# A gated-attention and FFN block on one core: a new opening that computes all six modulation rows, with both halves of x loaded ahead of the first two modulation matrices

## What is computed

```python
mod = (silu(c) @ wmod).reshape(4, 6, 1, 512)
sa, ca, ga, sb, cb, gb = (mod[:, i] for i in range(6))
ga, gb = ((2 * (g >= 0) - 1) * maximum(abs(g), 0.25) for g in (ga, gb))
h = layernorm(x) * (1 + ca) + sa
x = x + ga * attention(h)
h = layernorm(x) * (1 + cb) + sb
x = x + gb * (silu(h @ w_gate.T) * (h @ w_up.T)) @ w_down.T
```

## Time and profile before

| what | value |
|---|---|
| runs | 1098.33, 1099.9, 1103.17 us |
| the profiled execution's own time | 1100.45 us |
| its span, first to last instruction | 1098.7 us |
| busy in the span | PE 1045.7, DVE 816.6, ACT 696.6, POOL 224.2 us |
| first `scores` of the loop | 78.58 us from the start |
| first transpose of the FFN stage | 897.18 us from the start |
| DMA | 70.89 MB, 65 GB/s over the span |

### The profile page before, as it was taken

How to read it: one execution, slowest core, us unless ns; L and a number is a source line. 1 busy time by engine, 2 the same in 40 slices (tenths; PEclk the granted TensorE clock), 3 DMA queues, 4 the chain that set the end, 5 groups by cost and what they waited for, 6 DMA issues and landing times. The chain is left out here.

```text
span 1098.7 us, 14605 instructions
## 1 busy us (share of the span) xinstructions
PE 1045.7 (95%) x4680; PEld 808.4 (74%) x4680; DVE 816.6 (74%) x1585; ACT 696.6 (63%) x1368; POOL 224.2 (20%) x140
## 2 busy tenths in 40 slices
PE   5879999999999999999999999999997859999898
PEld 1657777777777777877777777787774349888786
DVE  5777887888888788878888887887878785444412
ACT  3448877887787788778878787877874434222300
POOL 3412212222211131122222112211323410000000
PEclk9989999999999999999999999999998969999999
DMA  6122301310131122013101311220123231111011
GB/s 226 55 67 80 112 20 38 100 53 19 38 115 39 33 85 91 19 38 115 38 19 38 126 44 40 77 76 19 45 72 135 76 129 45 57 38 58 29 39 38
DMA packets 37464, 70.89 MB, mean 65 GB/s; under 512 B 2936, under 2 KB 19576, under 8 KB 35520
## 3 DMA queue, kind: packets, MB, share of 16 engines
q1 hardware_dynamic: 36720, 70.16, 19.8%
q10 hardware_dynamic: 720, 0.43, 0.1%
HBM read 68.33 MB, written 2.24 MB: 64 GB/s over the span
## 5 line engine op out<-in xcount | busy, mean ns | idle before, releaser
L1373 POOL TENSOR_TENSOR q_sin<-q_sin,cst 128x512 f32<-128x512 f32 x64 | 88.9, 1388 | 311.7 <-ACT q_sin L764 311.7
L1213 DVE SCALAR_TENSOR_TENSOR prob<-ps_s,scal,dec 128x128 f32<-128x128 f32 x256 | 71.9, 343 | 77.6 <-PE ps_s L670 77.6
L1361 POOL TENSOR_TENSOR dec<-dec,future 128x1024 f32<-128x1024 f32 x31 | 74.5, 2402 | 265.9 <-ACT expg L783 265.9
L54 PE MATMUL ps_q<-hT_hi,wq_hi 128*128 128x512 f32 x256 | 125.5, 490 | 3.3 <-DVE q_cos L1023 2.5
L54 PE MATMUL ps_o<-wo_hi,z_hi 128*128 128x512 f32 x260 | 103.8, 399 | 2.5 <-DVE z_lo L49 2.4
L54 PE MATMUL ps_gt<-hT_hi,wg_hi 128*128 128x512 f32 x256 | 103.8, 405 | 2.0 <-DVE sg L1043 2.0
L56 PE MATMUL ps_o<-wo_hi,z_lo 128*128 128x512 f32 x260 | 103.4, 398 | 0.0
L55 PE MATMUL ps_o<-wo_lo,z_hi 128*128 128x512 f32 x260 | 103.2, 397 | 0.0
L56 PE MATMUL ps_q<-hT_hi,wq_lo 128*128 128x512 f32 x256 | 101.2, 395 | 0.0
L55 PE MATMUL ps_gt<-hT_lo,wg_hi 128*128 128x512 f32 x256 | 101.1, 395 | 0.0
L56 PE MATMUL ps_gt<-hT_hi,wg_lo 128*128 128x512 f32 x256 | 100.7, 393 | 0.0
(11 more groups left out here) (251 smaller groups left out, 2737.6 us busy)
## 6 DMA issues: line engine op xcount, KB each, us to landing
dec<-gT_dram SPq DMA_DIRECT2D x32, 512.0 KB, 5.5
raw_q<-wq_in SPq DMA_DIRECT2D x32, 256.0 KB, 2.7
raw_g<-wg_in SPq DMA_DIRECT2D x32, 256.0 KB, 2.9
raw_o<-wo_in SPq DMA_DIRECT2D x8, 1024.0 KB, 6.9
raw_pair<-wkv_in SPq DMA_DIRECT2D x8, 512.0 KB, 4.7
raw_pair<-wgu_in SPq DMA_DIRECT2D x6, 512.0 KB, 3.2
raw_gu<-wgu_in SPq DMA_DIRECT2D x5, 512.0 KB, 3.4
qT<-wmod_in SPq DMA_DIRECT2D x2, 1024.0 KB, 6.9
```

Source lines behind the costliest of these rows:

```text
L54: pe.matmul(out, w_hi, x_hi, start=first, stop=False)
L1213: last = nc.vector.scalar_tensor_tensor(prob[:, h], ps_s[:, h * P:(h + 1) * P], scal[:, tile, 1, h:h + 1], dec[:, tile // 2 % 2, h, tile % ...
L1361: nc.gpsimd.tensor_tensor(cells, cells, future[:].unsqueeze(1).broadcast_to([P, GRP * CPB, CHUNK]), ALU.add).then_inc(mask_done, 1)
L1373: nc.gpsimd.tensor_tensor(q2, q2, sinT, ALU.mult).then_inc(qsin_done, 1)
```

## The change

The tail's four rows and `guard_gate` go, and all six rows are made in the opening, in the order SA, CA, SB, CB, GA, GB. Each of a row's four k slices goes to its own strip of 32 result partitions; ACT copies the whole 128 x 512 bank, and `mod_turn` multiplies it with a 128 x 4 selector, which sums the strips and turns them. The norm works by batches: one ACT instruction covers both tiles of a batch, lower parts of batches 0 and 1 are made by POOL, of 2 and 3 by DVE. Heads 0 to 3 get own buffers (`raw_first`), their upper parts go to ACT, their lower parts stay on DVE. The two softplus products stand ahead of the first q block, and the whole softplus series stands ahead of `gate(0, -4)`. The zeroing of the output weights (3.7 us in the profile, L1379 to L1381) and of x1 by POOL stands behind the heads' splits and the last row. ga is stored and x reloaded before POOL needs them. The gates are stored to HBM element by element.

```diff
@@ SP
             sp.dma_start(cT, cT_in).then_inc(c_loaded, 16)
-            for half, m in enumerate((SA, CA)):
-                load_mod(m)
-                a = half * NT // 2
-                sp.dma_start(x1[:, a:a + NT // 2], ...
+            load_x(0)
+            load_x(1)
+            load_mod(SA)
+            load_mod(CA)
             load_kv(0)
-            load_head(0, 0, True)
+            load_first(0)
             sp.dma_start(cst[:, C_COST:C_TRI], cst_in[:, C_COST:C_TRI]).then_inc(tables_loaded, 16)
-            for j in range(1, GRP):
-                load_head(0, j)
+            load_first(1)
+            load_mod(SB)
+            load_mod(CB)
+            load_first(2)
+            load_first(3)
+            sp.wait_ge(ln_turned, B)
+            load_mod(GA)
+            load_mod(GB)
...
+            sp.wait_ge(guard, GUARD_END)
+            for i in range(2):
+                sp.dma_start(modrow[i].rearrange("(m p) -> p m", p=P),
+                             gate_T[:, i].rearrange("p b k -> p (b k)"),
+                             allow_slow_non_contiguous=True).then_inc(rows_stored, 16)
...
                     step(g, t, False, True, False)
                     sp.wait_ge(zz_done, g * 8 + 4)
-                    load_mod(CB)
-                    load_mod(SB)
+                    (loads both halves of x_again)
@@ PE
+            def mod_rows(m):
+                pe.wait_ge(mod_loaded[m], 16)
+                for k in range(KT):
+                    nc.tensor.matmul(ps_rows[m][k * LANE:(k + 1) * LANE], silu_c[:, k], wmod[m][:, k],
+                                     start=True, stop=True).then_inc(rows_ready, 1)
+            def mod_turn(slot, count):
+                pe.wait_ge(rows_copied, count)
+                part = mod_part[(count - 1) % 2]
+                for k in range(KT):
+                    last = nc.tensor.matmul(ps_modT[:, slot, k], part[:, k * P:(k + 1) * P], sel,
+                                            start=True, stop=True)
+                last.then_inc(mod_turned, 1)
...
+            mod_rows(SA); mod_rows(CA)
+            ln_turn(0); mod_turn(0, 1); mod_turn(1, 2); ln_turn(1)
+            kv_chunk(0, -1, 0); ln_turn(2); kv_chunk(0, -1, 1); ln_turn(3)
+            softplus_argument(0); softplus_argument(1)
+            q_block(0, -4, True); k_turn(0, -1); g_block(0, -4, 0, KT, True)
+            softplus_turn()
+            q_block(0, -3); mod_rows(SB); mod_turn(2, 3)
+            g_block(0, -3, 0, KT); mod_rows(CB); mod_turn(3, 4)
+            cumulative()
+            q_block(0, -2); mod_rows(GA); mod_turn(4, 5)
+            g_block(0, -2, 0, KT); mod_rows(GB); mod_turn(5, 6)
+            q_block(0, -1); g_block(0, -1, 0, KT)
@@ PE tail
-                    mod_row(GA)
-                    mod_row(CB)
-                    mod_row(GB)
-                    mod_row(SB)
-                    mod_turn(ps_late_modT, late_rows, 4)
@@ ACT, order from the first keys on
+            copy_zT(0); copy_v(0, -1); copy_zT(1)
+            swap(0, -4, True); copy_kT(0, -1); exp_gate(0, -4)
+            nc.scalar.activation(za, za, ACT.Exp, scale=-1.0)
+            sigmoid(0, -4); first_hi(2); swap(0, -3)
+            copy_rows(SB); exp_gate(0, -3); sigmoid(0, -3)
+            copy_rows(CB); first_hi(3); (copies of cumulative's results)
+            swap(0, -2); copy_rows(GA); exp_gate(0, -2); sigmoid(0, -2); copy_rows(GB)
@@ DVE, order from the norm on
+            ln_hi_half(0); split_kv_hi(0); split_kv_lo(0)
+            ln_tile_stats(6); ln_tile_stats(7); ln_variance(3)
+            ln_normalise(2); ln_hi_half(1); ln_normalise(3); first_lo(0)
+            for b in range(2, B):
+                ln_hi_half(b)
+                ln_lo_half(b)
+            split_v_lo(0, -1); rotate_k(0, -1); first_lo(1)
+            rotate_q_cos(0, -4); softplus_before_exp(); rotate_q_add(0, -4); cap(0, -4)
+            softplus_argument_of_series(); softplus_series(0); softplus_series(1)
+            gate(0, -4); decay_rates(); first_lo(2)
+            rotate_q_cos(0, -3); late_modT(2, 0.0); rotate_q_add(0, -3); cap(0, -3); gate(0, -3)
+            late_modT(3, 1.0); chunk_end(); first_lo(3)
+            (the same for -2, then state_weight, copy_scalars, guard_gates, the mask, then -1)
@@ DVE tail
-                    guard_gate(0)
-                    guard_gate(1)
@@ POOL
+            for t in range(-4, -1):
+                rotate_q_sin(0, t)
+            pool.wait_ge(wh_split, GRP)
+            (zeroes wo_hi, wo_lo)
+            pool.wait_ge(rows_ready, KT * len(MODS))
+            nc.gpsimd.memset(x1[:], 0.0).then_inc(zeros_done, 1)
+            rotate_q_sin(0, -1)
+            def residual_tile(t):
+                pool.wait_ge(sums_done, KVH * NT - (NT - 1) + t + 1)
+                scale_sum(nc.gpsimd, 0, t)
+                add_x(nc.gpsimd, pool, 0, t, t)
```

More of the change, by code:

```diff
@@ L39 @@
 SA, CA, GA, SB, CB, GB = range(6)
+MODS = (SA, CA, SB, CB, GA, GB)
 def split_hi(engine, hi, full):
@@ L418, in load_mod, with load_x, load_first, load_head @@
             def load_mod(m):
[L419 to L427, removed]
+                sp.dma_start(wmod[m], wmod_in[m]).then_inc(mod_loaded[m], 16)
+            def load_x(half):
+                a = half * NT // 2
+                sp.dma_start(x1[:, a:a + NT // 2], x_in[a:a + NT // 2].rearrange("t p n -> p t n"))\
+                    .then_inc(x_loaded[half], 16)
+            def load_first(j):
+                sp.dma_start(raw_first[:, j, 0], wq_in[j]).then_inc(first_loaded[j], 16)
+                sp.dma_start(raw_first[:, j, 1], wg_in[j]).then_inc(first_loaded[j], 16)
+            def load_head(g, j):
+                sp.wait_ge(wh_split, g * 4 + j)
                 sp.dma_start(raw_q[:], wq_in[bass.ds(g * 4 + j, 1)].rearrange("o p k d -> (o p) k d"))\
@@ new lines, in mod_turn, with ln_turn @@
+                last.then_inc(mod_turned, 1)
+            def ln_turn(b):
+                pe.wait_ge(ln_xn, CPB * (b + 1))
+                if b >= 2:
+                    pe.wait_ge(ln_hf, b - 1)
+                for c in range(CPB):
+                    for k in range(KT):
+                        last = nc.tensor.transpose(pairs[b % 2][:, c, k * P:(k + 1) * P],
+                                                   x1[:, b * CPB + c, k * P:(k + 1) * P], ident)
+                last.then_inc(ln_turned, 1)
@@ new lines, in _ @@
+            scalar_rstd(2)
+            first_hi(0)
+            scalar_rstd(3)
+            modulate(2)
+            modulate(3)
+            first_hi(1)
+            copy_zT(0)
+            copy_v(0, -1)
+            copy_zT(1)
+            swap(0, -4, True)
+            copy_kT(0, -1)
+            exp_gate(0, -4)
+            act.wait_ge(chain, CHAIN_ABS)
+            nc.scalar.activation(za, za, ACT.Exp, scale=-1.0).then_inc(exp_done, 1)
+            sigmoid(0, -4)
+            first_hi(2)
@@ L859, in _ @@
+            swap(0, -2)
+            copy_rows(GA)
+            exp_gate(0, -2)
+            sigmoid(0, -2)
+            copy_rows(GB)
+            act.wait_ge(chain, CHAIN_DIFF)
+            nc.scalar.activation(zs, zs, ACT.Exp).then_inc(exp_done, 1)
+            act.wait_ge(mod_turned, 6)
+            exp_g(0, -1)
+            swap(0, -1)
+            decays(0, 0)
+            exp_gate(0, -1)
+            sigmoid(0, -1)
             act.wait_ge(gT_stored, 32)
@@ L1157, in _ @@
[L1157 to L1166 removed]
+            ln_tile_stats(6)
@@ new lines, in _ @@
+            first_lo(1)
+            rotate_q_cos(0, -4)
+            softplus_before_exp()
+            rotate_q_add(0, -4)
+            cap(0, -4)
+            softplus_argument_of_series()
+            softplus_series(0)
+            softplus_series(1)
+            gate(0, -4)
+            decay_rates()
+            first_lo(2)
+            rotate_q_cos(0, -3)
+            late_modT(2, 0.0)
+            rotate_q_add(0, -3)
+            cap(0, -3)
+            gate(0, -3)
+            late_modT(3, 1.0)
@@ new lines, in _ @@
+            chunk_end()
+            first_lo(3)
+            rotate_q_cos(0, -2)
+            rotate_q_add(0, -2)
+            cap(0, -2)
+            gate(0, -2)
+            state_weight()
+            copy_scalars(0, -1, True)
+            guard_gates()
+            dve.wait_ge(expg_done, 1)
+            dve.wait_ge(future_done, 2)
+            cells = dec[:, 0].rearrange("p h c i -> p (h c) i")
+            nc.vector.tensor_tensor(cells, cells,
+                                    future[:].unsqueeze(1).broadcast_to([P, GRP * CPB, CHUNK]),
+                                    ALU.add).then_inc(mask_done, 1)
@@ L1205, in _ @@
+            rotate_q_cos(0, -1)
+            rotate_q_add(0, -1)
+            cap(0, -1)
             dve.wait_ge(zeros_done, 1)
```

505 lines of the change are left out of this document (241 added, 264 removed).

## The result

The changed kernel took 1123.8 us (median of 4 runs, 1122.65 to 1125.59) against 1099.1 of the kernel before on the same chips: ratio 1.0222, 95% interval 1.0187 to 1.0257. The forecast was 1108.5, the range ended at 1118.

The account below looks back on a forecast made before the run. PE is busy throughout the loop, so only the opening and the last group's tiles 4 to 7 could move time: 1100.45 + 9.4 - 1.0 = 1108.9, forecast as 1108.5 us; own range 1105.5 to 1113, wide range 1098 to 1118.

Parts of the forecast that it names:

- wide range: Whole kernel: 1098 to 1118 us, taking in rivals of a break-even opening and serial strips, and the unknowns' ends.
- own range: Whole kernel: the forecast's narrower range, 1105.5 to 1113 us around 1108.5.
- Leg 1: Opening, from 0 to the first modulation: wmod[CA] lands later, strips run together; modulation at 21.6, 1.9 us later than before.
- rival 3: Row strips run one after the other instead of beside each other: +6 us, 1114.5; chance 0.17.
- Leg 2: Opening, up to the softplus turn: wkv_lo ends at 28.0 against 24.65 before; chain ends at 48.7 us.
- Leg 3: Opening, up to g_block(0, -3): it waits for gate(0, -4) behind the whole series, starts at 58.2; PE idles some 5 us.
- Leg 4: Opening, up to the end of cumulative: gate block, CB's selector product after ACT, cumulative sums; ends at 67.7 us.
- Leg 5: Opening, up to scores: remaining q and gate blocks, rows GA and GB; 18.1 us, ending at 85.8.
- my term for it: Opening: matmuls at the lower clock behind three waits of 2 us or more, 2.2 us; scores at 88.0.
- The zeroing of x1: Opening, near the cap of t = -2: POOL's zeroing may add up to 3 us, left to the range.
- Tail: Last group's tiles 4 to 7: taken rows return 3.0 us, lower clock costs 2.0, net -1.0; ends -5 to +2.
- Rival 4: Element-wise gate stores hold the queue: +5 us in the loop's first steps, 1113.9; chance 0.08.

Follow-up runs that it names:

- a1: Kernel before with 32 unused bytes a partition behind the constants table, moving the left SBUF tensors up 32 bytes; 1110.0 us, ratio 1.0077.
- a2: Changed kernel with 224 unused bytes a partition behind the constants table, restoring left tensors' addresses modulo 256; 1113.9 us, ratio 1.0118 to before.
- m1: Matmuls alone in the kernel's shapes, weights and moving operand each at four addresses 32 bytes apart; 226.9 to 234.3 ns from start to start.
- b1: a2 plus unneeded matmuls in PE's waits in the opening; 1112.2 us, ratio 1.0122 to the kernel before.
- c2: c1 with each late selector product behind the next block of products and the fillers ahead of them gone; 1112.1 us, ratio 1.0102 to before.
- d4: c1 without rows SB, CB, GA, GB, their copies, selector products and the gates' bound, ones instead; 1106.8 us, ratio 1.0067 to before.
- c3: Kernel before plus unneeded matmuls in its own PE waits in opening and tail; 1098.0 us, ratio 0.9976.
- b4: a2 plus unneeded matmuls in PE's waits in the last group's tiles 4 to 7; 1107.1 us, ratio 1.0075 to the kernel before.
- d1: c2 with gate stores on ACT's queue, x1 zeroed behind the cap of t = -2, z 128 bytes higher; 1106.2 us, ratio 1.0061 to before.
- e2: d1 with the two element-wise gate stores issued by SP in the last group's first step; 1098.9 us, ratio 0.9995 to the kernel before.
- b2: a2 with gate(0, -4) on DVE moved ahead of the softplus series; 1117.3 us, ratio 1.0166 to the kernel before.
- c1: a2 with the gate order of b2, tail fillers of b4 and fewer opening fillers than b1; 1105.4 us, ratio 1.0052 to the kernel before.

## Why the prediction was wrong, step by step

- **"... the loop's instructions are the same after the change, so it can move the time only through the opening ..., the last group's tiles 4 to 7 ... and nothing behind": this step failed.** The same instructions ran 5.3 us slower in the loop and 5.1 in the FFN stage, because their operands had moved by 32 bytes (a1, a2, m1). Without them the time is a2's 1113.9: inside the wide range, 5.4 above the forecast and 0.9 above the end of its own range.
- Leg 1 held: modulation at 21.97 (21.6). Four matmuls of a row run beside each other: 1.06 us warm against 3.60, 3.4 times; rival 3 is out. The Trainium skill ("TensorE: Matmul & The Clock Gate", Part 3, "Measured speedup vs the span model") has 2.38 times for three strips; no run here has three, and four gave more.
- Leg 2 held: wkv_lo ended at 28.52 (28.0), the softplus turn began at 48.81 (48.7). Its sum enters 2.6 for a lower part priced at 2.4; that changes nothing.
- Leg 3: g_block(0, -3) at 59.56 (58.2), behind gate(0, -4) with 4.5 us of idle PE around the selector product. The six series operations took 3.78, not some 2.7. The sum itself is loose here: it enters 1.3 for operations listed with 1.2 and 0.4, and adds the 0.9 that it calls beside; from the turn to the argument's first operation (48.81 to 51.59) it was 2.8 instead of these 2.2.
- Leg 4: 11.7 us instead of 9.5. The gate block ran 4.6 instead of 2.8 at the lower clock; the rest fits.
- Leg 5: 22.3 instead of 18.1: the last q block 5.3 instead of 2.8, the selector product 1.4 instead of 0.8, small terms more. Low clock in legs 4 and 5 was 5 us by these rows and 4.7 by b1, and my term for it 2.2: the largest mis-sized term of the opening, half of its 5.6 over the forecast.
- The zeroing of x1, left to the range at up to 3, missed the cap in the changed kernel by 0.1 us; that it cost nothing was luck. It made the cap 4.8 (c2) and 6.1 (d4) longer where it met it.
- Tail: the mechanism was right, both sizes were not. With fillers in both kernels the tail is 67.8 (c3) and 62.1 (b4), so the rows and their collateral were worth 5.7 us, not 3.0 (of that up to 2.4 is row CB at the lower clock, 5.97 for 3.60). The lower clock cost the changed kernel 7.2 (5.4 against a2) and the kernel before 1.7, so the change added 5.5 (3.7), not 2.0. That -0.3 lies near the forecast's -1.0 is luck: two errors of like size cancel. By the Trainium skill's rule ("TensorE: Matmul & The Clock Gate", "Loop structure matters more than you think") I had +2.2; the trace agrees with the rule's direction, output and square-sum products at 0.77 behind waits of 3 to 6 us, and b4 shows the price.
- Rival 4's mechanism exists (c2, d1, e2), its price was zero here, 1.7 us in b1 and 5.7 in c2, whose openings are shorter.

## What to carry to other kernels

"The same instructions" are the same only if their operands stay where they were: after any edit to a buffer's size, compare the length of a stretch that should not change first. Work that is taken out of PE's waits can be paid back in clock unless something else keeps PE busy. A change in order should be tried together with such fillers: b2 alone looked like a loss of 3.4 us, and with them (c1) it was none. Before two openings are compared, look whether PE's first products ran at the same clock level in both.

## What the runs showed of the hardware that I had not expected

- A 512-column matmul follows the one before after 227 ns where weights and moving operand have the same address modulo 256 (3 of 16 pairs tried), after 229 at one of the four pairs that are 64 apart, and after 232 to 234 at the other 12 (m1).
- DVE's TENSOR_SCALAR on SBUF waited out POOL's memsets to the end of the last of several in a row: 0.43 us became 5.2 (c2) and 6.6 (d4).
- Two element-wise stores of 2048 values each took 13 to 20 us to land, and a 512 KB load issued behind them 14 to 21 instead of 5, on another engine's queue as well (changed kernel, b1, c2, d1).
